# Two more weight blocks in vacated homes, a third layout of homes, and a rearranged first expert round

## The chip, the cores and the metric

One core of one Trainium2 chip runs the whole kernel in one launch. The metric is the device time of that core in microseconds (us), the median of several executions. The kernel before takes 501.85 us in the median of three (500.89 to 502.28).

## The reference

A graph attention network of two layers over 128 nodes of 768 features (4096 edges and a self-loop for each node), and after it a mixture of eight experts with a small tridiagonal solve at the end. Everything is float32. Cut to what matters here:

```python
h   = gat_conv(layernorm(x), W1 [768 x 6144], 8 heads)      # then elu
x   = x + gat_conv(elu(h), W2 [6144 x 768], 1 head)
xn  = layernorm(x)
probs = softmax(xn @ Wg + bg);  top_p = max(probs);  comb = one_hot(argmax(probs)) * top_p
h   = gelu(einsum('bnd,edh->ebnh', xn, W1) + b1)              # 8 experts, 768 x 3072 each
y   = einsum('ebnh,ehd->ebnd', h, W2) + b2                    # 8 experts, 3072 x 768 each
ffn = einsum('ebnd,bne->bnd', y, comb)
v   = clip(ffn @ Wv + bv); mask = scores >= 12th largest score; (gr, gi) = diagonal of a tridiagonal inverse of v
out = x + ffn + bk_scale * (clip(stack(gr, gi) * mask) @ Wo + bo)
```

The weights are some 190 MB and each is used once.

## The kernel before

The weights pass through SBUF in blocks. The GNN's come as 32 blocks of 1152 KB (`slot`), through a ring of nine slots. Each of the eight experts is a **round** of 14 blocks: six blocks of W1, 128 rows of 3072 numbers (1536 KB, index 0 to 5, the "upper" ones), and eight of W2 (1152 KB, index 6 to 13, the "lower" ones). A place in SBUF where a block lands is called a home.

**Homes.** While the GNN still runs, nothing but its ring and what it no longer needs is to be had, so the first round (round 0) has a layout of its own: `chunks` (chunk0 to chunk5) and `lowers` (lower0 to lower7, eight of the nine ring slots). From the second round (round 1) on there is another: `chunks_on` is three homes outside that area (extra0 to extra2) and chunk0 to chunk2, and `lowers_on` is three homes cut from chunk3 to chunk5 and then lower0 to lower4. So lower5, lower6 and lower7 fall vacant when round 0 is over. The kernel before puts rows and small tiles for the end of the program there.

**Who issues.** All weights are requested by SyncE's DMA queue (SPq), in program order. Ahead of each request SyncE waits on the semaphore `used`, which TensorE raises once for each block that it has read: by 32 over the GNN, and then by 14 a round. `used_after(r)` is 32 + 14 r. `load_round(r, e, first)` requests the blocks from `first` on of round r, and block i waits for `used` to reach `used_after(r - 1) + i + 1 - first`. For round 1, whose blocks 0 to 2 go to the extras ahead of that, `first` is 3: block 3 waits for the first block of round 0 to be read, and the last, 13, for the eleventh. For rounds 2 to 7 `first` is 0: block 0 of a round waits until TensorE has read block 0 of the round before.

```python
load(1, 1, 2, moe_in, chunks_on, lowers_on)
load_round(1, 1, first=3)
with sp.Fori(2, ROUNDS) as r:
    load_round(r, r)
```

**TensorE in a round.** `up(k)` multiplies block k of W1 by the gathered nodes (`gathered`, up to 64 nodes of that expert) into PSUM banks 0 to 2; ScalarE copies these to `upper`; `turn_upper(q)` transposes a quarter; VectorE adds the bias (`add_bias`), ScalarE takes the gelu; `down(q)` multiplies with two lower blocks into bank 4. `used` goes up at the end of up(0) to up(4), for block 5 at the first transpose of turn_upper(0), and at the end of each lower block. Beside that stand `gather` (it collects the nodes of the next expert), a transpose of `place_top` and `scatter` (it adds the last round's result into banks 6 and 7).

Round 0 has its own order, as the routing of nodes to experts is still being worked out in it: between its up's stand the rank products, the second half of the first gather, the turn of the scores, of `hot_top` (for `first_ffn`, the experts' b2) and of `place_top`. All this is in `round_(0, first=True)` of each engine. Between the GNN and round 0 TensorE has a chain of small steps with VectorE and ScalarE (second attention, sum, layer norm, gate). `stay_warm(n)` are n products of 128 x 128 that nobody reads, and `WARM` holds their numbers; `WARM[3]` are those ahead of the turn of the second attention's weights.

Of the kernel before, what the change touches and what calls it, by code (L numbers as in the profile page):

```python
# [19 lines left out]
P = 128  # L20
# [37 lines left out]
WARM = (3, 5, 2, 2, 2, 0, 1, 3, 2, 0, 8, 12)  # L58


def gnn_moe_kernel(nc, x, src, dst, gw1, gas1, gad1, gb1, gw2, gas2, gad2, gb2,
# [7 lines left out]
    with ctx:  # L69
        ctx.enter_context(nc.allow_non_contiguous_dma(reason="the gate's columns, 768 words each"))  # L70

        def sem(name):
            return ctx.enter_context(nc.semaphore(name))
# [51 lines left out]
        junk = nc.alloc_sbuf_tensor_at("junk", [P, D], f32, offset=moe_base + lower_at[5])  # L125
        top[0] = moe_base + lower_at[6]
        wo_rows = place("wo_rows", [P, 2, D])
        wv_row = place("wv_row", [P, D])
        top[0] = moe_base + lower_at[7]
# [9 lines left out]
        assert top[0] <= moe_base + lower_at[7] + slot  # L139
# [21 lines left out]
        chunks_on = [extra0, extra1, extra2] + chunks[0:3]  # L161
# [72 lines left out]
        lead_in = [sem(f"lead_in{i}") for i in range(LOADS)]  # L234
        up_done = sem("up_done")
# [63 lines left out]
        def _(sp):  # L299
# [35 lines left out]
            def load_round(r, e, first=0):  # L335
                for i in range(first, LOADS):
                    sp.wait_ge(used, used_after(r - 1) + i + 1 - first)
                    load(r, e, i, moe_in, chunks_on, lowers_on)

            for n in range(GNN_HALVES):  # L340
# [12 lines left out]
                if n == 22:  # L353
                    sp.wait_ge(spread, HEADS + 1)
                    sp.wait_ge(bias_done, 1)
                    sp.wait_ge(hot_ready, 4)
                    load(1, 1, 1, moe_in, chunks_on, lowers_on)
# [7 lines left out]
                if n == 25:  # L365
                    sp.wait_ge(x_based, 1)
                    load(1, 1, 0, moe_in, chunks_on, lowers_on)
# [27 lines left out]
        def _(pool):  # L395
# [51 lines left out]
            pool.wait_ge(used, used_after(0) + LOADS)  # L447
# [25 lines left out]
        def _(act):  # L473
# [67 lines left out]
            act.wait_ge(hot_turned, 1)  # L541
            S.copy(hot_T[:, :], ps[0:EXPERTS, 7, 0:P]).then_inc(hot_T_ready, 1)

            def round_(r, first=False):
# [8 lines left out]

                if not first:
                    take_y(r)
                act.wait_ge(place_turned, r + 1)
                S.copy(place_T[:, :], ps[:, 5, HB:512]).then_inc(place_T_ready, 1)
                for s in range(3):
                    take_upper(s)
                for q in range(QU):  # L560
                    gelu(q)

# [18 lines left out]
        def _(dve):  # L581
# [299 lines left out]
            def round_(r, first=False):  # L881
                def add_bias(q):
# [8 lines left out]
                dve.wait_ge(place_turned, r + 1)  # L891
                V.tensor_scalar(place_top[:, :], slot_no[:, :, :].rearrange("p a j -> p (a j)"),  # L892
                                rank[:, bass.ds(r + 1, 1)], col(TOPP), ALU.is_equal, ALU.mult)
                V.tensor_scalar(place_now[:, :], slot_no[:, 0, :], rank[:, bass.ds(r + 1, 1)], col(RSTD),
                                ALU.is_equal, ALU.mult).then_inc(place_ready, 1)
# [121 lines left out]
        def _(pe):  # L1017
# [239 lines left out]
            def round_(r, first=False):  # L1257
                upper_homes, lower_homes = (chunks, lowers) if first else (chunks_on, lowers_on)

                def landed(i):  # L1260
                    if first:
                        pe.wait_ge(lead_in[i], 16)
                    else:
                        pe.wait_ge(moe_in[i], 16 * r)
# [40 lines left out]
                if first:  # L1305
                    pe.wait_ge(first_gathered, 1)
                    up(0)
                    pe.wait_ge(onehot_ready, 1)
                    T.matmul(ps[:, 7, 16:24], later[:, :], hot, start=True, stop=True).then_inc(rank_done, 1)
                    T.matmul(ps[:, 6, 16:24], ones[:, :], hot, start=True, stop=True).then_inc(rank_done, 1)  # L1310
                    gather_first(3, KT, 5)
                    pe.wait_ge(first_gathered, 2)
                    up(1)
# [5 lines left out]
                    up(2)  # L1319
                    first_ffn()  # L1320
                    pe.wait_ge(first_gathered, 3)
                    up(3)
                    pe.wait_ge(thr_ready, 1)
                    T.transpose(ps[:, 5, HB:512], place_top[:, :], ident[:, :]).then_inc(place_turned, 1)
                    up(4)
                    up(5)
                else:
                    pe.wait_ge(gathered_ready, r)
                    up(0)
                    scatter(r)  # L1330
                    up(1)
                    up(2)
                    T.transpose(ps[:, 5, HB:512], place_top[:, :], ident[:, :]).then_inc(place_turned, 1)  # L1333
                    for k in range(3, KT):
                        up(k)
# [9 lines left out]
                if first:  # L1345

                    T.matmul(ps[:, 3, HB:HB + 1], ones[0:1, :], top16[0:1, KEEP - 1:KEEP], start=True,
                             stop=True).then_inc(thr_done, 1)
# [15 lines left out]
            with pe.Fori(1, rounds) as r:  # L1364
                round_(r)
# [63 lines left out]
```

## Time and profile before

| | |
|---|---|
| median of three executions | 501.85 us (500.89 to 502.28) |
| the profiled execution, its time | 502.62 us |
| its span in the trace | 500.8 us |
| TensorE busy | 466.2 us, 93% |
| VectorE, ScalarE, GpSimd busy | 136.2, 62.1, 32.9 us |
| read from HBM | 189.62 MB, 379 GB/s over the span |
| the weights' queue, share of 16 DMA engines | 93.2% |

The time exceeds the span by 1.8 us, which lie around the first and the last instruction. TensorE's busy share says little by itself: a product that waits for a semaphore behind its weight load, or whose end is modelled, counts as busy. What a DMA moved in each stretch is the more telling column here.

### The profile page before, as it was taken

To read this page: it belongs to the slowest core of one execution; us is meant where nothing else is said; L and a number is where in the kernel's file an instruction comes from. 1 tells how busy PE (TensorE), PEld (TensorE's weight loads), DVE (VectorE), ACT (ScalarE), POOL (GpSimd) and SP (SyncE) were. 2 spreads that over 40 slices of the span, in tenths; PEclk is the share of its full clock that TensorE was granted. 3 is DMA by queue.
4 is the path that set the end of the run, shared out by engine and by line. 5 is a ranking of instruction groups with operands and counts; after the bars stand their busy time and mean duration, and the time that the engine had idled before them with its cause. 6 is when DMAs were issued, how large, how long until landed. Compare 5 with 4: busy or idle time off the path is not lost.

```text
span 500.8 us, 5998 instructions
## 1 busy us (share of the span) xinstructions
PE 466.2 (93%) x2292; PEld 232.7 (46%) x2292; DVE 136.2 (27%) x362; ACT 62.1 (12%) x119; POOL 32.9 (7%) x52
## 2 busy tenths in 40 slices
PE   7999999999998999999999999999898889789892
PEld 6666665666556344344344344353243234224352
DVE  6673697437105311010010010010010011001165
ACT  1010222002003120020020020020020011002100
POOL 3242220000100000121000000000000000000000
PEclk9999999999998999999999999999999999999996
DMA  8889999999999699899999999999999999999800
GB/s 309 309 285 403 402 401 417 413 401 411 426 425 370 237 407 375 338 417 420 425 428 423 422 427 427 423 421 430 424 424 424 425 425 423 425 425 424 347 1 31
DMA packets 32541, 190.22 MB, mean 380 GB/s; under 512 B 5423, under 2 KB 5631, under 8 KB 18190
## 3 DMA queue, kind: packets, MB, share of 16 engines
q1 hardware_dynamic: 31694, 189.94, 93.2%
q8 instruction: 9, 0.15, 0.1%
q0 software_dynamic: 544, 0.05, 0.1%
q10 hardware_dynamic: 288, 0.03, 0.0%
q14 instruction: 6, 0.05, 0.0%
HBM read 189.62 MB, written 0.39 MB: 379 GB/s over the span
## 4 chain that ended last, share of the span: by engine, by line
PE 58%; DMA 22%; SPq 13%; DVE 5%; issue 2%; ACT 0%; DVEq 0%
PE ps L1300 16%; DMA chunk<-in_L_ffn_W 14%; PE ps L1273 14%; PE ps L1099 11%; PE ps L1059 6%; DMA lower<-in_L_ffn_W 6%; SPq L333 5%; SPq L323 4%; SPq L328 3%; PE ps L1286 2%; PE ps L1087 2%; DMA slot<-in_L_gnn_W 2%; PE ps L1114 2%; PE ps L1235 2%; SPq L347 1%
## 5 line engine op out<-in xcount | busy, mean ns | idle before, releaser
L1300 PE MATMUL ps<-lower,hidden 128*64 128x384 f32 x516 | 88.6, 490 | 5.3 <-DMA lower<-in_L_ffn_W 5.3
L1273 PE MATMUL ps<-chunk,gathered 128*64 128x512 f32 x324 | 73.5, 598 | 7.3 <-DMA chunk<-in_L_ffn_W 7.3
L1059 PE MATMUL ps<-slot,xT 128*128 128x384 f32 x192 | 64.0, 487 | 0.2 <-DMA slot<-in_L_gnn_W 0.2
L1273 PE MATMUL ps<-extra,gathered 128*64 128x512 f32 x252 | 57.6, 597 | 6.1 <-DMA extra<-in_L_ffn_W 5.9
L1300 PEld LDWEIGHTS ps<-lower,hidden 128*64 128x64 f32 x516 | 35.9, 137 | 51.2 <-issue 40.6
L1099 PE MATMUL ps<-slot,eluT 128*128 128x384 f32 x168 | 55.3, 486 | 0.0
L884 DVE TENSOR_TENSOR hidden<-ps,b_T 128x384 f32<-128x384 f32 x32 | 17.1, 555 | 129.8 <-PE ps L1286 129.8
L1059 PEld LDWEIGHTS ps<-slot,xT 128*128 128x128 f32 x192 | 35.6, 190 | 22.8 <-issue 0.3
L1273 PEld LDWEIGHTS ps<-chunk,gathered 128*64 128x64 f32 x324 | 21.7, 136 | 50.6 <-issue 36.7
L1300 PE MATMUL ps<-lower_on,hidden 128*64 128x384 f32 x252 | 43.7, 492 | 0.0
L1099 PEld LDWEIGHTS ps<-slot,eluT 128*128 128x128 f32 x168 | 31.5, 190 | 20.7
L892 DVE TENSOR_SCALAR place_top<-slot_no,rank,small 128x128 f32<-128x128 f32 x8 | 2.8, 346 | 130.6 <-PE ps L1333 126.5
L1273 PEld LDWEIGHTS ps<-extra,gathered 128*64 128x64 f32 x252 | 16.9, 136 | 42.5 <-issue 29.9
L551 ACT ACTIVATE hidden<-hidden 128x384 f32<-128x384 f32 x32 | 16.3, 523 | 79.7 <-DVE hidden L884 79.7
L1300 PEld LDWEIGHTS ps<-lower_on,hidden 128*64 128x64 f32 x252 | 16.9, 136 | 18.8 <-issue 17.5
L547 ACT COPY upper<-ps 128x512 f32<-128x512 f32 x24 | 14.0, 585 | 57.8 <-PE ps L1273 57.8
L1286 PEld LDWEIGHTS ps<-ident,upper 128*128 128x128 f32 x96 | 12.8, 199 | 16.1 <-issue 9.6
L658 DVE CUSTOM_DVE_ANT_0 xc<-h_sb,att_rows 128x768 f32<-128x768 f32 x16 | 16.5, 1033 | 9.6 <-issue 5.6
L1029 PE MATMUL ps<-ident 128*128 128x128 f32 x82 | 15.2, 343 | 2.9 <-DVE ident L601 2.9
L1286 PE MATMUL ps<-ident,upper 128*128 128x128 f32 x96 | 17.4, 304 | 0.0
L1029 PEld LDWEIGHTS ps<-ident 128*128 128x128 f32 x82 | 13.8, 253 | 4.0 <-DVE ident L601 2.9
L493 ACT ACTIVATE elu_e<-elu_e 128x384 f32<-128x384 f32 x16 | 8.4, 523 | 42.6 <-DVE elu_e L694 42.6
(303 smaller groups left out, 287.1 us busy)
## 6 DMA issues: line engine op xcount, KB each, us to landing
lower<-in_L_ffn_W SPq DMA_DIRECT2D x43, 1152.0 KB, 23.1
chunk<-in_L_ffn_W SPq DMA_DIRECT2D x27, 1536.0 KB, 19.7
slot<-in_L_gnn_W SPq DMA_DIRECT2D x31, 1152.0 KB, 15.6
extra<-in_L_ffn_W SPq DMA_DIRECT2D x21, 1536.0 KB, 25.1
lower_on<-in_L_ffn_W SPq DMA_DIRECT2D x21, 1152.0 KB, 28.7
slot<-in_L_gnn_W SPq DMA_DIRECT2D x3, 384.0 KB, 4.8
x_sb<-in_x SPq DMA_DIRECT2D x1, 384.0 KB, 3.4
out<-xc SPq DMA_DIRECT2D x1, 384.0 KB, 2.3
```

Of the source, the lines that this page charges most:

```text
L323: sp.dma_start(target, view).then_inc(small_in, 16)
L328: sp.dma_start(upper_homes[i][:, :], w1[e, i * P:(i + 1) * P, :]).then_inc(landed[i], 16)
L333: sp.dma_start(lower_homes[i - CHUNKS][:, :, :], view).then_inc(landed[i], 16)
L551: S.activation(hidden[:, q, :, :, :], hidden[:, q, :, :, :], ACT.Gelu_apprx_tanh).then_inc(gelu_done, 1)
L658: dot = V.tensor_tensor_reduce(out=xc[:, :], in0=h_sb[:, h, :], in1=att_rows[:, h % 2, j, :], scale=1.0, scalar=0.0, op0=ALU.mult, op1=ALU ...
L884: V.tensor_tensor(hidden[:, q, :, :, :], ps[:, q, 0:HB].rearrange("p (k b j) -> p k b j", k=3, b=2), b1_T[:, bass.ds(r, 1), :] .rearrange( ...
L1029: T.matmul(ps[:, bank, 0:P], ident[:, :], ident[:, :], start=True, stop=True)
L1059: last = T.matmul(ps[:, 2 * (h % 2) + b, 0:HB], xT[:, 3 * half + k, :], slots[n % RING][:, k, b * HB:(b + 1) * HB], start=(n % 2 == 0 and ...
L1099: last = T.matmul(ps[:, b, 0:HB], elu_part(KT * h + 3 * half + k, 1)[:, 0, :], slots[n % RING][:, k, b * HB:(b + 1) * HB], start=(h == 0 a ...
L1273: last = T.matmul(ps[b * CAP:(b + 1) * CAP, s, 0:BANK], gathered[:, k, :], upper_homes[k][:, at:at + BANK], start=(k == 0), stop=(k == KT ...
L1286: last = T.transpose(ps[:, q, k * P:(k + 1) * P], upper[:, q * HB + k:(q + 1) * HB:3], ident[:, :])
L1300: last = T.matmul(ps[c * CAP:(c + 1) * CAP, 4, 0:HB], hidden[:, q, k, b, :], lower_homes[i][:, k, c * HB:(c + 1) * HB], start=(i == 0 and ...
```

## The change

Five things.

1. `left0` and `left1`, two homes of 1536 KB, are laid over lower5, lower6 and two thirds of lower7, and SyncE requests blocks 0 and 1 of round 2 into them as soon as `used` reaches `used_after(1) - 1` and `used_after(1)`, the last two reads of round 0. The rest of round 2 (`load_round(2, 2, first=2)`) then waits two reads less for each block than before.
2. From round 2 on there is a third layout: upper homes left0, left1, extra0 to extra2, chunk0; lower homes `lower_late0` and `lower_late1` (cut from chunk1 and chunk2), the three cut from chunk3 to chunk5, and lower0 to lower2. What falls vacant is lower3 and lower4, after round 1, and the tiles for the program's end move there; GpSimd starts on them a round later. From round 3 on a round's block i waits again for block i of the round before.
3. Round 1, with the second layout and semaphores of its own (`second_in`), is written out apart from the loop on TensorE and SyncE.
4. Round 0 is rearranged on TensorE, VectorE and ScalarE: gather's second half ahead of up(1), the ranks ahead of up(2), the score ahead of up(3); the turns of `place_top` and `hot_top`, the gather for round 1 and `first_ffn` go behind down(0) and down(1), and all four `turn_upper` ahead of down(0).
5. `WARM[3]` is 8 and was 2.

The lines of the diff that the text speaks of:

```diff
-WARM = (3, 5, 2, 2, 2, 0, 1, 3, 2, 0, 8, 12)
+WARM = (3, 5, 2, 8, 2, 0, 1, 3, 2, 0, 8, 12)
...
+        left = [nc.alloc_sbuf_tensor_at(f"left{i}", [P, HID], f32, offset=moe_base + lower_at[5] + i * 4 * row)
+                for i in range(2)]
...
-        chunks_on = [extra0, extra1, extra2] + chunks[0:3]
+        chunks_2nd = [extra0, extra1, extra2] + chunks[0:3]
+        lowers_2nd = lowers_on
+        chunks_on = left + chunks_2nd[0:4]
+        lowers_on = [nc.alloc_sbuf_tensor_at(f"lower_late{i}", [P, 3, D], f32, offset=moe_base + chunk_at[1 + i])
+                     for i in range(2)] + lowers_2nd[0:6]
...
-            load(1, 1, 2, moe_in, chunks_on, lowers_on)
-            load_round(1, 1, first=3)
-            with sp.Fori(2, ROUNDS) as r:
+            load(1, 1, 2, second_in, chunks_2nd, lowers_2nd)
+            load_round(1, 1, second_in, chunks_2nd, lowers_2nd, first=3)
+            for i in range(2):
+                sp.wait_ge(used, used_after(1) - 1 + i)
+                load(2, 2, i, moe_in, chunks_on, lowers_on)
+            load_round(2, 2, first=2)
+            with sp.Fori(3, ROUNDS) as r:
                 load_round(r, r)
...
-            pool.wait_ge(used, used_after(0) + LOADS)
+            pool.wait_ge(used, used_after(1) + LOADS)
...
+                if not first:
+                    next_place()
                 add_bias(0)
                 add_bias(1)
-                take_gathered(r + 1, 5)
+                if not first:
+                    take_gathered(r + 1, 5)
                 add_bias(2)
+                add_bias(3)
                 if first:
+                    next_place()
+                    take_gathered(1, 5)
                     take_threshold()
-                add_bias(3)
...
-                    pe.wait_ge(gathered_ready, r)
-                    up(0)
...
+                    up(2)
...
+                    pe.wait_ge(first_gathered, 3)
+                    for k in range(3, KT):
+                        up(k)
+                    for q in range(QU):
+                        turn_upper(q)
+                    pe.wait_ge(thr_ready, 1)
+                    down(0)
                     pe.wait_ge(top_ready, 1)
+                    T.transpose(ps[:, 5, HB:512], place_top[:, :], ident[:, :]).then_inc(place_turned, 1)
+                    down(1)
...
+                    pe.wait_ge(place_ready, 2)
+                    pe.wait_ge(place_T_ready, 1)
+                    gather(5)
                     first_ffn()
-                    pe.wait_ge(first_gathered, 3)
-                    up(3)
...
+                    down(2)
+                    down(3)
```

On TensorE, in the middle of round 0, the kernel before has the following order. `chunk_69` to `chunk_72` are the upper blocks 2 to 5, `lower_73` and `lower_74` the first two lower blocks; `place_now` marks the gather, `b_sb,hot_T` `first_ffn`, `ident,upper` the turns.

```order
L1315 MATMUL ps<-ident,small 1x128
L1317 MATMUL ps<-ident,hot_top 8x128
L1273 MATMUL ps<-chunk_69,gathered 64x512 x6
L1254 MATMUL ps<-b_sb,hot_T 128x384 x2
L1273 MATMUL ps<-chunk_70,gathered 64x512 x6
L1324 MATMUL ps<-ident,place_top 128x128
L1273 MATMUL ps<-chunk_71,gathered 64x512 x6
L1273 MATMUL ps<-chunk_72,gathered 64x512 x6
L1286 MATMUL ps<-ident,upper 128x128 x6
L1235 MATMUL ps<-place_now,x_120 128x64 x6
L1300 MATMUL ps<-lower_73,hidden 64x384 x6
L1300 MATMUL ps<-lower_74,hidden 64x384 x6
```

After the change the same engine has, from the same product of the scores on:

```order
L1342 MATMUL ps<-ident,small 1x128
L1299 MATMUL ps<-chunk_70,gathered 64x512 x6
L1299 MATMUL ps<-chunk_71,gathered 64x512 x6
L1299 MATMUL ps<-chunk_72,gathered 64x512 x6
L1312 MATMUL ps<-ident,upper 128x128 x12
L1326 MATMUL ps<-lower_73,hidden 64x384 x6
L1326 MATMUL ps<-lower_74,hidden 64x384 x6
L1351 MATMUL ps<-ident,place_top 128x128
L1326 MATMUL ps<-lower_75,hidden 64x384 x6
L1326 MATMUL ps<-lower_76,hidden 64x384 x6
L1353 MATMUL ps<-ident,hot_top 8x128
L1258 MATMUL ps<-place_now,x_122 128x64 x6
```

The upper blocks 3 to 5 and the first lower blocks have moved ahead of `hot_top`, `place_top`, the gather and `first_ffn`. Nothing was added between them.

On SyncE, at the seam of round 1 and round 2, the kernel before has the last requests of round 1 and then those of its loop, each behind a wait for `used` (the ISA and REGISTER_ALU rows are the loop's register work):

```order
L333 DMA lower_76<-in_L_ffn_W 128x2304
L333 DMA lower_77<-in_L_ffn_W 128x2304
L381 UNCONDITIONAL_BRANCH
L381 ISA
L328 ISA
L328 DMA extra_119<-in_L_ffn_W 128x3072
L337 REGISTER_ALU
L328 ISA
L328 DMA extra_116<-in_L_ffn_W 128x3072
L337 REGISTER_ALU
L328 ISA
```

And after the change:

```order
L340 DMA lower_76<-in_L_ffn_W 128x2304
L340 DMA lower_77<-in_L_ffn_W 128x2304
L335 DMA left_84<-in_L_ffn_W 128x3072
L335 DMA left_85<-in_L_ffn_W 128x3072
L335 DMA extra_121<-in_L_ffn_W 128x3072
L335 DMA extra_118<-in_L_ffn_W 128x3072
L335 DMA extra_139<-in_L_ffn_W 128x3072
L335 DMA chunk_67<-in_L_ffn_W 128x3072
L340 DMA lower_late_140<-in_L_ffn_W 128x2304
L340 DMA lower_late_141<-in_L_ffn_W 128x2304
```

The two homes `left_84` and `left_85` now stand behind the last request of round 1, and the extras have become the third to fifth home of round 2.

## Rows read from the trace of the kernel before

**Rows 1.** The page, 40 slices of 12.5 us: GB/s that the DMA engines moved

```profile
GB/s 309 309 285 403 402 401 417 413 401 411 426 425 370 237 407 375 338 417 420 425 428 423 422 427 427 423 421 430 424 424 424 425 425 423 425 425 424 347 1 31
```

**Rows 2.** Stretches: length, busy times of PE, PEld, DVE, ACT, POOL, PEclk, DMA share, GB/s

```profile
155.16:158.58 3.42, 3.35 (x13) 2.18 (x11) 2.24 (x6) 1.85 (x5) 0.39 (x1) 0.50 0.99 361
157.00:170.00 13.00, 12.93 (x77) 7.87 (x77) 4.89 (x28) 3.49 (x9) 0.60 (x1) 0.94 0.69 253
170.00:195.00 25.00, 25.00 (x135) 10.91 (x133) 6.20 (x20) 3.76 (x8) 0.00 (x0) 1.00 0.94 360
195.00:204.00 9.00, 9.00 (x54) 3.59 (x50) 0.00 (x0) 0.77 (x2) 2.01 (x10) 1.00 0.97 407
204.00:216.00 12.00, 12.00 (x57) 4.00 (x57) 0.57 (x2) 0.27 (x1) 2.79 (x11) 1.00 0.90 347
240.00:316.00 76.00, 76.00 (x414) 31.39 (x414) 6.53 (x14) 9.06 (x18) 0.00 (x0) 1.00 1.01 426
316.00:445.00 129.00, 114.49 (x604) 44.55 (x600) 9.80 (x21) 13.60 (x27) 0.00 (x0) 1.00 1.01 424
```

**Rows 3.** The page, requests of one kind: count, KB each, median us to landing

```profile
lower<-in_L_ffn_W SPq DMA_DIRECT2D x43, 1152.0 KB, 23.1
chunk<-in_L_ffn_W SPq DMA_DIRECT2D x27, 1536.0 KB, 19.7
```

**Rows 4.** SyncE's requests in time: start, us from first to last, line, home

```profile
156.62 0.33 SPq L328 DMA_DIRECT2D extra<-in_L_ffn_W  x1
...
165.19 7.57 SPq L328 DMA_DIRECT2D chunk<-in_L_ffn_W  x3
176.63 6.19 SPq L333 DMA_DIRECT2D lower_on<-in_L_ffn_W  x3
186.45 9.76 SPq L333 DMA_DIRECT2D lower<-in_L_ffn_W  x5
204.41 6.46 SPq L328 DMA_DIRECT2D extra<-in_L_ffn_W  x3
...
237.86 0.33 SPq L333 DMA_DIRECT2D lower<-in_L_ffn_W  x1
...
240.45 0.34 SPq L328 DMA_DIRECT2D extra<-in_L_ffn_W  x1
```

**Rows 5.** TensorE ahead of the second attention's turn: start, us, what, [idle before]

```profile
151.21 0.61 PE L1029 MATMUL ps<-ident 128*128 128x128 f32 x4
153.46 0.33 PE L1076 MATMUL ps<-ident,att_p 128*128 128x128 f32 x1 [1.64 <-DVE small L782]
```

**Rows 6.** Pieces of the chain that ended last, in time: start, us, what

```profile
154.55 2.05 PE ps L1210 x4
...
157.30 0.90 PE ps L1021 x3
...
162.42 2.73 PE ps L1273 x12
...
165.69 0.72 PE ps L1242 x6
...
172.39 1.48 PE ps L1254 x4
...
183.04 1.29 PE ps L1235 x12
184.33 4.02 PE ps L1300 x24
188.35 0.54 PE ps L1286 x3
...
201.65 2.57 PE ps L1273 x12
```

**Rows 7.** The page, groups in the rounds: busy us, mean ns of one, idle before

```profile
L884 DVE TENSOR_TENSOR hidden<-ps,b_T 128x384 f32<-128x384 f32 x32 | 17.1, 555 | 129.8 <-PE ps L1286 129.8
L551 ACT ACTIVATE hidden<-hidden 128x384 f32<-128x384 f32 x32 | 16.3, 523 | 79.7 <-DVE hidden L884 79.7
```

More of the change, by code:

```diff
@@ L138, in gnn_moe_kernel @@
          cf_d, cf_c, cf_g, cf_e, cf_f, cf_pre, cf_px, cf_sx) = [place(*t) for t in tail_tiles]
-        assert top[0] <= moe_base + lower_at[7] + slot
+        assert top[0] <= moe_base + lower_at[4] + slot
         top[0] = after_moe
@@ L234, in gnn_moe_kernel @@
         lead_in = [sem(f"lead_in{i}") for i in range(LOADS)]
+        second_in = [sem(f"second_in{i}") for i in range(LOADS)]
         up_done = sem("up_done")
@@ L552, in gelu, with turn_place @@
                                  ACT.Gelu_apprx_tanh).then_inc(gelu_done, 1)
+                def turn_place():
+                    act.wait_ge(place_turned, r + 1)
+                    S.copy(place_T[:, :], ps[:, 5, HB:512]).then_inc(place_T_ready, 1)
                 if not first:
                     take_y(r)
-                act.wait_ge(place_turned, r + 1)
-                S.copy(place_T[:, :], ps[:, 5, HB:512]).then_inc(place_T_ready, 1)
+                    turn_place()
                 for s in range(3):
@@ L561, in round_ @@
                     gelu(q)
+                if first:
+                    turn_place()
+                    act.wait_ge(hot_turned, 1)
+                    S.copy(hot_T[:, :], ps[0:EXPERTS, 7, 0:P]).then_inc(hot_T_ready, 1)
             def take_y(n):
@@ L1255, in first_ffn, with round_ @@
                              start=True, stop=True)
-            def round_(r, first=False):
-                upper_homes, lower_homes = (chunks, lowers) if first else (chunks_on, lowers_on)
+            def round_(r, first=False, second=False):
+                upper_homes, lower_homes = ((chunks, lowers) if first else (chunks_2nd, lowers_2nd) if second
+                                            else (chunks_on, lowers_on))
                 def landed(i):
@@ L1262, in landed @@
                         pe.wait_ge(lead_in[i], 16)
+                    elif second:
+                        pe.wait_ge(second_in[i], 16)
                     else:
-                        pe.wait_ge(moe_in[i], 16 * r)
+                        pe.wait_ge(moe_in[i], 16 * r - 16)
                 def up(k):
@@ new lines, in round_ @@
+                    down(3)
+                    T.matmul(ps[:, 3, HB:HB + 1], ones[0:1, :], top16[0:1, KEEP - 1:KEEP], start=True,
+                             stop=True).then_inc(thr_done, 1)
+                    return
+                pe.wait_ge(gathered_ready, r)
+                up(0)
+                scatter(r)
+                up(1)
+                up(2)
+                T.transpose(ps[:, 5, HB:512], place_top[:, :], ident[:, :]).then_inc(place_turned, 1)
+                for k in range(3, KT):
+                    up(k)
@@ L1344, in round_ @@
                 turn_upper(3)
-                if first:
-                    T.matmul(ps[:, 3, HB:HB + 1], ones[0:1, :], top16[0:1, KEEP - 1:KEEP], start=True,
-                             stop=True).then_inc(thr_done, 1)
                 down(2)
@@ L1363, in _ @@
             rounds = pe.value_load(route[0:1, 0:1], min_val=ROUNDS, max_val=ROUNDS + 1)
-            with pe.Fori(1, rounds) as r:
+            round_(1, second=True)
+            with pe.Fori(2, rounds) as r:
                 round_(r)
```

45 lines of the change are left out of this document (16 added, 29 removed).

## The prediction, made before the changed kernel ran

> **What bounds the kernel now.** I read first what the DMA engines moved over the 40 slices [rows 1]. From slice 17 to 37 they move 417 to 430 GB/s without a break: the weights come as fast as this trace ever shows. So a byte that moves earlier ahead of that stretch ends the stream earlier, and the last expert's products and the final solve hang on the stream's end. Time is lost where the line of requests was short: in the first three slices (309, 309, 285), which the change leaves alone, and in slices 13 to 16 (370, 237, 407, 375, 338), between the GNN and the second expert round.
>
> Then the stretches [rows 2], counted against 425 GB/s: 157 to 170 us moves 253, a loss of 13 x (1 - 253/425) = 5.3 us; 170 to 195 moves 360, 3.8 us; 195 to 204 moves 407, 0.4 us; 204 to 216 moves 347, 2.2 us. Together 11.7 us. TensorE shows no idle in 158 to 216, so it is not waiting for weights; the weights wait for homes, which TensorE frees. Later, from 240 to 316 us, both columns are full (426 GB/s, TensorE 76.00 of 76.00) and from 316 on TensorE has pauses while the DMA does not: by then the stream alone decides. The requests in time [rows 4] show the holes: after 156.62 none until 165.19, and after 196.21 (186.45 + 9.76, less 0.33 for the start of the last: 195.88) none until 204.41, which is the first block of round 2, waiting for the first read of round 1.
>
> **An account of the stream.** An upper block of 1536 KB (1.573 MB) takes 3.70 us at 425 GB/s, a lower one of 1152 KB (1.180 MB) 2.78 us [rows 3]. I let a block start when the one ahead is through, but not sooner than 1.5 us after its request, and feed it with the 13 requests from 156.62 to 204.41 [rows 4], the line being empty at 157.1 us. Its idle time is 1.0 us after 156.62, 4.9 before the block of 165.19, 1.8 in small holes from 169 to 196 and 4.1 before that of 204.41, 11.8 in all against the 11.7 measured. The 1.5 us is my choice to make the two agree; with 1.0 it gives 11.3, with 2.1 12.4. It places the loss less well than it sums it: it has 1.8 us in the middle where the rows have 3.8, and more at both ends.
>
> **Part 1, the six warm products.** TensorE sits idle for 1.64 us ahead of the turn of the second attention, and its granted clock then is 0.50, the 1.2 GHz level, from 155.16 to 158.58 [rows 2, 5]. Two warm products show as x4 and span 0.61 us, so six more take at most 1.8 us (the 0.61 holds a start-up that further ones in a queue need not pay): they fill the idle time and end as the weights arrive, at worst 0.2 us late. At the full level the two products of 384 columns take 1.48 us (L1254, same shape of result) and not 2.05, and three turns 0.54 and not 0.90 [rows 6]. That is 0.57 + 0.36 = 0.9 us on the chain that leads to round 0. Bounds: nothing if the clock falls anyway, 1.7 us if all of the 3.42 us were products. I take 0.9, from the rows of the two groups on the chain.
>
> The Trainium skill ("TensorE: Matmul & The Clock Gate", Part 1 on the clock gate) says that the gate watches activity in a window that runs free of the kernel, and that the point of change therefore differs between runs. By that rule the filled gap need not help in each run, which is a rival below; this trace shows only one instance, at 155.16.
>
> **Part 2, the new order of round 0.** The pieces of the chain [rows 6] give the times of reads. up(0) moves from 162.42 to 161.5; each up is 2.73 or a little less, gather's half 0.72, `first_ffn` 1.48, the gather 1.29, a pair of lower blocks 4.02, the turn of a quarter 0.54 at most. The two rank products together, the score, and the turns of `place_top` and `hot_top` I take at 0.5, 0.3, 0.3 and 0.2, small products like the warm ones, of which two span 0.61 [rows 5]. In the new order SyncE's requests, each at the end of a read, come at 164.3, 167.8, 171.1, 174.1, 176.8, 179.7 (block 5), 183.2, 185.2, 187.4, 189.4 and 194.4 (block 10), where block 5 had been at 182.5 and block 10 at 195.9 [rows 4] (a span there ends 0.33 us after its last request goes out). The same work is done, so the round ends at about 200.7, 0.9 earlier than 201.65. Only the requests in between are 2 to 3.5 us earlier, because `first_ffn`, the gather and the two turns (1.48 + 1.29 + 0.5 us) now stand behind them.
>
> What could wait in it: down(0) follows the turns at once, with no gather between. The first bias (0.56 us) and gelu (0.52 us) [rows 7] need 1.1 us and two hand-offs after the first quarter is turned; the other three quarters are turned meanwhile, 1.4 to 1.6 us, so this costs 0 to 0.3 us. If that cover were gone, it would cost the whole 1.1. The vector work on the ranks, the top probability and the twelfth score, short steps on 128 x 8 and 1 x 128 numbers, has the up's of blocks 2 to 5 (11 us) to hide behind. I take nothing.
>
> **Part 3, two more homes.** Round 0's blocks 12 and 13 are read at about 198.3 and 200.3; the requests for left0 and left1 go out then, and the extras follow at 203.3, 206.8, 209.4. Before, they were 204.41 and two more by 210.9 [rows 4]. So the request at the hole comes 6.1 us earlier. In the account the middle has no idle left (before 1.8), the hole keeps 0.7 us (before 4.1), and the first part is 5.0 (before 5.9, as the earlier chain brings both requests forward). The line is never empty after that.
>
> Sum: 5.0 + 0 + 0.7 = 5.7 us of idle time where 11.8 was, a gain of 6.1. The rows bound it: if the middle gives 1.8 and the hole only what the rows show there, 0.4 + 2.2 - 0.7 = 1.9, it is 0.5 + 1.8 + 1.9 = 4.2 (and with the smaller 0.5 for the first part); with 3.8 in the middle and 3.4 at the hole it is 0.9 + 3.8 + 3.4 = 8.1. With only one or two blocks in line the rate is somewhat under 425 (the middle's 360 was not all holes), and the new middle is still such a stretch. So I take 5.7.
>
> **Part 4, what costs nothing.** The later start of GpSimd's end work (some 36 us later, still over 200 us ahead of the end) is off every path. TensorE's round 1, written out, has the same products. From round 3 on each request waits as before.
>
> The profiled execution would go from 502.62 to 496.9 us (span 500.8 to 495.1); it lies 0.8 above the median of the runs shown, so the median would be 501.85 - 5.7 = **496.1 us**.
>
> **The rivals.**
> *The clock falls all the same* (or falls at another place of this chain). For it: the fall is seen once, and the gap is filled only just. Then 0.9 us of the chain stays; in the account the idle time is 6.6, the gain 5.2, less the same 0.4: 497.0 us.
> *Round 0 pauses.* The new order brings products nearer to the vector and scalar work that they need. Each us ahead of block 0 or before the hole costs a whole us, since the line is empty there. 2 to 4 us of it give 498 to 500 us. Against it: the covers above.
> *Nothing is gained.* That takes another limit: homes scarce again at the next seam. TensorE reads a round in 36 us (201.65 to the like piece; requests 204.41 and 240.45 [rows 4]), a round's 18.9 MB takes 44.4 us. After the change no request goes out between the end of round 2's, at about 234, and the first of round 3, at about 239.3. The account's line is through at 244.2, so the new request is there (240.8 with its start) 3.4 us ahead of need; before it was 250.3 against 241.95. A margin of 3.4 us would have to go. That, or an unseen cap, would leave 501.9 us.
> *Slower.* One mechanism: ahead of block 0's read in round 0, where no cover exists, a stop of TensorE, such as warm products at the 1.2 GHz level that hold back the turn, or a wait for `gathered`'s second half ahead of up(1), which had a whole up to hide in and now has only up(0)'s end. The piece itself is 0.72 us and ScalarE's copy a fraction. It must exceed 5.7 us to decide, and 7.2 to be over 0.3% slower, ten times what these rows hold; it would give 503 to 505 us.
>
> **How the numbers follow.** Forecast 0.64 (its own range 494.4 to 497.8, from the bounds 4.2 and 8.1 drawn in to 7.5); clock 0.22; pause 0.08; nothing 0.04; slower 0.02. The range 494.5 to 498.2 holds the first two nearly whole. About 0.3% (1.5 us) is what a measurement can tell from no change. Faster by that: 0.64 + 0.22 + 0.08 = 0.94; within it 0.04; slower 0.02.
>
> **What would show it.** In the profile after: granted clock 1.00 in 155 to 159; requests at about 179.7 (block 8 of round 1), 194.4 and 198.3; a first hole of GB/s still there at 162 to 166, the middle over 400, and the hole at 203 to 206 gone; the stream's end some 5.7 us earlier. What would make me wrong: a middle that stays at 360 to 380 GB/s although requests come earlier, or waits in front of down(0).

## The result, and the profile after

The changed kernel takes 497.91 us in the median of six executions (496.13 to 498.67), the kernel before beside it 501.94 (six, 500.89 to 502.28). The ratio is 0.9913 with a 95% interval of 0.9901 to 0.9926: 4.0 us faster, and clear of no change. The profiled execution took 497.94 us with a span of 496.1; that of before had 502.62 and 500.8, so the two traces lie 4.7 us apart and not 4.0.

The page of the changed kernel, GB/s in 40 slices (here of 12.4 us), to be held against [rows 1]:

```profile
GB/s 292 332 274 403 401 401 414 413 405 409 426 424 412 291 401 398 384 429 418 424 422 423 426 427 425 424 424 424 424 424 427 427 421 425 425 426 424 338 0 32
```

The same stretches as in [rows 2]: length, busy PE, PEld, DVE, ACT, POOL, granted clock, DMA share, GB/s.

```profile
155.16:158.58 3.42, 3.26 (x23) 2.36 (x23) 2.02 (x6) 1.83 (x5) 0.60 (x1) 1.00 1.03 396
157.00:170.00 13.00, 13.00 (x77) 7.24 (x77) 3.64 (x25) 2.77 (x8) 0.60 (x1) 1.00 0.75 290
170.00:195.00 25.00, 24.85 (x133) 11.13 (x131) 6.14 (x19) 4.19 (x9) 0.00 (x0) 0.96 1.00 411
195.00:204.00 9.00, 9.00 (x52) 3.77 (x50) 0.45 (x2) 0.48 (x1) 0.00 (x0) 0.93 0.91 327
204.00:216.00 12.00, 12.00 (x57) 3.75 (x55) 0.57 (x2) 0.27 (x1) 0.00 (x0) 1.00 1.01 430
240.00:316.00 76.00, 76.00 (x414) 31.15 (x412) 6.53 (x14) 9.07 (x18) 5.19 (x17) 1.00 1.01 424
```

Against 425 GB/s the losses are now 13 x (1 - 290/425) = 4.1 us, 0.8, 2.1 and -0.1, 6.9 in all where before they were 11.7. The difference, 4.8 us, is the 4.7 us of the two spans: the whole gain lies between 157 and 216 us. It arrives at the other end through the stream: the products of the very last lower block wait for their DMA in both kernels, and start 4.71 us earlier (first row before, second after). From there both traces have 25.3 us more.

```profile
475.53 2.16 PE L1300 MATMUL ps<-lower,hidden 128*64 128x384 f32 x12 [0.51 <-DMA lower<-in_L_ffn_W]
470.82 2.16 PE L1326 MATMUL ps<-lower,hidden 128*64 128x384 f32 x12 [0.51 <-DMA lower<-in_L_ffn_W]
```

The middle has filled (360 to 411) and 204 to 216 is full; but 195 to 204, which before moved 407, moves 327. And the granted clock, 0.50 at 155 before and now 1.00 there, has another dent (a stretch at a lower granted clock), 0.96 and 0.93 further on.

SyncE's requests of the changed kernel around the two holes (start, us, line, home; each row is from a view of a short stretch):

```profile
155.83 0.33 SPq L335 DMA_DIRECT2D extra<-in_L_ffn_W  x1
163.92 0.33 SPq L335 DMA_DIRECT2D chunk<-in_L_ffn_W  x1
...
195.84 0.33 SPq L340 DMA_DIRECT2D lower<-in_L_ffn_W  x1
200.00 0.33 SPq L335 DMA_DIRECT2D left<-in_L_ffn_W  x1
201.93 0.33 SPq L335 DMA_DIRECT2D left<-in_L_ffn_W  x1
204.97 0.33 SPq L335 DMA_DIRECT2D extra<-in_L_ffn_W  x1
```

The homes are used as meant. Up to the middle the requests are 0.3 to 0.5 us ahead of the forecast (163.92 for 164.3); block 10's, block 12's and the extra's are 1.4, 1.7 and 1.7 us behind it (194.4, 198.3 and 203.3). What lies between them is in the chain of the changed kernel (start, us, what):

```profile
178.87 1.64 PE ps L1312 x12
180.50 0.15 issue
180.66 4.09 PE ps L1326 x24
184.75 0.26 PE ps L1351
185.01 4.02 PE ps L1326 x24
189.03 0.32 PE ps L1353 x2
189.34 1.48 PE ps L1258 x12
190.83 1.48 PE ps L1277 x4
192.31 9.59 PE ps L1326 x48
```

The last row is down(2) and down(3), blocks 10 to 13. By [rows 6] two such blocks take 4.02 us, four about 8; here they take 9.59. A stretch within it gives the reason:

```profile
193.00:196.00 3.00, 3.00 (x12) 1.23 (x10) 0.00 (x0) 0.00 (x0) 0.00 (x0) 0.50 1.00 421
```

TensorE runs at the 1.2 GHz level (0.50) from 193 to 196 us although it shows no idle time. Ahead of it stand the turn of `hot_top`, the gather (products of 64 columns) and `first_ffn` (8 rows of the array in use), which the new order has put next to each other. Whether they cause the fall is for the experiments.

### The profile page after: what moved, and what is told of

It is laid out like the page before. It is cut to its first block, busy times and chain, and to the rows that moved or that the text cites. A ratio compares the mean times of both kernels' runs of the same rounds, so it can differ in the third digit from the quotient of the medians.

```text
span 496.1 us, 5969 instructions
## 1 busy us (share of the span) xinstructions
PE 465.3 (94%) x2304; PEld 232.8 (47%) x2304; DVE 135.7 (27%) x362; ACT 62.0 (13%) x119; POOL 32.9 (7%) x52
## 4 chain that ended last, share of the span: by engine, by line
PE 73%; DMA 12%; SPq 6%; DVE 6%; issue 2%; ACT 0%; POOL 0%; DVEq 0%; POOLq 0%
PE ps L1326 19%; PE ps L1299 19%; DMA lower<-in_L_ffn_W 12%; PE ps L1082 11%; PE ps L1122 11%; SPq L340 6%; PE ps L1312 2%; PE ps L1110 2%; PE ps L1258 2%; PE ps L1137 2%; PE ps L1052 1%; PE ps L1388 1%; PE ps L1044 0%; DVE elu_y L708 0%; DVE cf_w L954 0%
## 5 line engine op out<-in xcount | busy, mean ns | idle before, releaser
L1326 PE MATMUL ps<-lower,hidden 128*64 128x384 f32 x372 | 65.2, 499 | 4.9 <-DMA lower<-in_L_ffn_W 4.7
L1326 PEld LDWEIGHTS ps<-lower,hidden 128*64 128x64 f32 x372 | 26.9, 139 | 40.6 <-issue 31.7
L1299 PE MATMUL ps<-chunk,gathered 128*64 128x512 f32 x180 | 40.8, 596 | 1.8 <-DMA chunk<-in_L_ffn_W 1.8
L1299 PE MATMUL ps<-left,gathered 128*64 128x512 f32 x144 | 33.3, 598 | 3.2 <-DMA left<-in_L_ffn_W 3.1
L1326 PE MATMUL ps<-lower_late,hidden 128*64 128x384 f32 x144 | 24.5, 490 | 0.0
L1299 PEld LDWEIGHTS ps<-chunk,gathered 128*64 128x64 f32 x180 | 12.3, 137 | 25.8 <-issue 21.9
L1299 PEld LDWEIGHTS ps<-left,gathered 128*64 128x64 f32 x144 | 9.6, 136 | 23.0 <-issue 17.3
```

The source lines that it names most:

```text
L1299: last = T.matmul(ps[b * CAP:(b + 1) * CAP, s, 0:BANK], gathered[:, k, :], upper_homes[k][:, at:at + BANK], start=(k == 0), stop=(k == KT ...
L1326: last = T.matmul(ps[c * CAP:(c + 1) * CAP, 4, 0:HB], hidden[:, q, k, b, :], lower_homes[i][:, k, c * HB:(c + 1) * HB], start=(i == 0 and ...
```

## The experiments

Theory: the stream of weights sets the time; it loses what TensorE's reads are late while its line is empty; the new order has a clock dent of its own that costs 1.7 us. The rivals: each part brings its own share wherever it stands; the shortfall against the account comes from a shallow line and not from the clock.

### The homes alone

The kernel before with edits 1 to 3 of the change and without 4 and 5:

```diff
-            with sp.Fori(2, ROUNDS) as r:
...
+            for i in range(2):
+                sp.wait_ge(used, used_after(1) - 1 + i)
+                load(2, 2, i, moe_in, chunks_on, lowers_on)
+            load_round(2, 2, first=2)
+            with sp.Fori(3, ROUNDS) as r:
```

> The kernel before with the extra homes and the third layout alone: round 0 in its old order, two warm products. If the gain is that of the hole ahead of round 2's first block, the first request for a left home goes out near 199.7 us and the second near 201.6 instead of 204.4, the stretch 204 to 216 moves over 420 GB/s and the middle (170 to 195) stays near 360. By the account of the stream that is 4.1 us less (11.8 to 7.7 us of idle time), by the rows of the hole at most 2.6: 497.8 to 499.3 us. Rival, that the new order is what matters and the homes only use what it frees: within 1 us of the kernel before.

Measured: 498.9 us (before beside it 502.0), ratio 0.9937 (0.9916 to 0.9958): 3.1 us. Stretches of this kernel, columns as above, and its requests for the left homes:

```profile
170.00:195.00 25.00, 25.00 (x137) 10.99 (x135) 5.69 (x17) 4.05 (x8) 0.00 (x0) 1.00 0.96 374
195.00:204.00 9.00, 9.00 (x52) 3.61 (x50) 0.00 (x0) 0.48 (x1) 0.00 (x0) 1.00 1.02 424
204.00:216.00 12.00, 12.00 (x57) 3.84 (x55) 0.57 (x2) 0.27 (x1) 0.00 (x0) 1.00 1.01 429
```

```profile
199.18 2.26 SPq L335 DMA_DIRECT2D left<-in_L_ffn_W  x2
```

The hole before round 2 is gone, the middle keeps most of its own. The gain falls between the rows' bound (2.6) and the account (4.1); its interval, 2.1 to 4.2 us, does not choose between them. Most of the change's 4.0 us is this part.

### The order alone

The changed kernel with the homes taken back. The eight warm products stay in it:

```diff
-        chunks_on = left + chunks_2nd[0:4]
-        lowers_on = [nc.alloc_sbuf_tensor_at(f"lower_late{i}", [P, 3, D], f32, offset=moe_base + chunk_at[1 + i])
-                     for i in range(2)] + lowers_2nd[0:6]
+        chunks_on = chunks_2nd
...
-            for i in range(2):
-                sp.wait_ge(used, used_after(1) - 1 + i)
-                load(2, 2, i, moe_in, chunks_on, lowers_on)
-            load_round(2, 2, first=2)
-            with sp.Fori(3, ROUNDS) as r:
+            with sp.Fori(2, ROUNDS) as r:
```

> The changed kernel without the extra homes: the new order of round 0 and the eight warm products stay, round 2's first block goes to its old home and waits again for round 1's first read. Theory: every earlier request only lets the line run dry earlier, since the stream can't restart before that read, which in the changed kernel comes at 205.0 us and before at 204.4. So it gives nothing or is up to 0.6 us slower than before: 501.5 to 502.5 us, middle over 400 GB/s, but a longer hole ahead of 205. Rival, that each part brings its own share: about 3.5 us less for the middle and 0.9 for the clock, near 498.

Measured: 502.33 us, ratio 1.0007 (0.9991 to 1.0022): no change. Its stretches:

```profile
170.00:195.00 25.00, 24.85 (x139) 11.55 (x139) 6.15 (x19) 4.20 (x9) 0.00 (x0) 1.00 0.99 405
195.00:204.00 9.00, 9.00 (x50) 3.44 (x48) 0.45 (x2) 0.48 (x1) 2.29 (x16) 1.00 0.57 218
```

The middle fills as in the changed kernel, and all of it is lost again behind it, most in 195 to 204 (218 GB/s), where no request goes out between these two:

```profile
193.65 0.33 SPq L336 DMA_DIRECT2D lower<-in_L_ffn_W  x1
202.64 0.36 SPq L331 DMA_DIRECT2D extra<-in_L_ffn_W  x1
```

Bytes moved earlier are worth something only if the line has others behind them. By the sum of [rows 2], the middle loses 1.2 us where it lost 3.8, and the stretches from 195 to 216 lose 5.2 where they lost 2.6.

This trace has the new order and no clock dent: its clock is 1.00 through all of round 0, and at 157 to 170 us it loses 3.5 us where the kernel before lost 5.3. Its span is 1.7 us under that of before, although the medians are the same. The twelve executions fall into two groups of six: 500.48 to 501.90 us with a mean granted clock of 0.989 to 0.992, the traced one among them, and 502.76 to 503.79 us with 0.987 or 0.988. So the dent probably comes in half of this kernel's executions; there is no trace of the second group, so this is not shown. The next experiment finds the warm products worth 1.0 us by themselves; here, with the order, nothing is left of that.

### The warm products: on the kernel before, and out of the changed one

```diff
-WARM = (3, 5, 2, 2, 2, 0, 1, 3, 2, 0, 8, 12)
+WARM = (3, 5, 2, 8, 2, 0, 1, 3, 2, 0, 8, 12)
```

> The kernel before with eight warm products instead of two, nothing else. Theory: in the kernel before the line restarts at the request that waits for round 1's first read (204.4 us), so whatever brings that read forward is gained whole: the clock stays 1.00 at 155, that request goes out near 203.1, and the time is 1.0 to 1.3 us less than before, near 500.8. Rival, that TensorE's chain ahead of round 0 is hidden behind the stream: no change.

Measured: 501.12 us beside 502.1, ratio 0.9982 (0.9972 to 0.9993): 1.0 us faster. The trace shows the clock at 1.00 around 155 and round 2's first request at 202.64 instead of 204.41 [rows 4]:

```profile
155.16:158.58 3.42, 3.25 (x26) 2.84 (x26) 1.94 (x7) 1.56 (x4) 0.60 (x1) 1.00 1.00 396
202.64 0.36 SPq L328 DMA_DIRECT2D extra<-in_L_ffn_W  x1
```

The request is 1.8 us earlier and the span 1.7 us shorter (499.1 for 500.8): nothing covers the chain ahead of round 0. The medians give less than the pair of traces. The traced execution of the kernel before has a mean granted clock of 0.985; of the 55 executions of it that ran beside the experiments 28 have 0.988 or less and take 502.2 us in the mean, 27 have 0.989 or more and take 501.3. So the fall at 155 seems to come in about half of them. This is a hint only, as the mean clock also counts falls near the program's end (0.78 from 484 to 488 us in the trace before).

The other way round, the changed kernel with `WARM[3]` at 2:

> The changed kernel with two warm products ahead of the second attention's turn instead of eight. Theory: TensorE then sits idle some 1.6 us there again, its granted clock is 0.5 for some 3.4 us around 155, the chain reaches round 0 0.9 to 1.3 us later, and since the line of requests is empty at 162 to 165 us and again ahead of the left homes, all of it is added: 1 to 1.3 us slower than the changed kernel, if the second fall (behind the gather) comes as in the changed kernel; if that one goes away, as the round lies elsewhere in time, the two nearly cancel. Rival, that the extra products only fill time: no difference, clock 1.00 at 155.

Measured: 497.37 us, ratio 0.9902 (0.9887 to 0.9918), against 497.91 and 0.9913 of the changed kernel: not slower, and the intervals overlap. The expectation's second branch came true: the request for left0 goes out at 199.87, in the changed kernel at 200.00. TensorE's wait and the clock's fall are back (timeline of TensorE, and a stretch), and the second dent is not there (chain):

```profile
153.74 0.33 PE L1099 MATMUL ps<-ident,att_p 128*128 128x128 f32 x1 [1.64 <-DVE small L798]
```

```profile
155.16:158.58 3.42, 3.35 (x11) 1.89 (x10) 2.48 (x7) 1.71 (x4) 0.00 (x0) 0.51 1.03 374
```

```profile
190.91 1.48 PE ps L1258 x12
192.39 1.48 PE ps L1277 x4
193.88 7.89 PE ps L1326 x48
```

Blocks 10 to 13 take 7.89 us here. So a dent costs 9.59 - 7.89 = 1.7 us of reads. The other traces that have these four blocks on end agree: 9.58 us with a dent (two repeats of the changed kernel), 7.89 without (four other kernels).

### Light pieces apart

`first_ffn` moved behind down(2) in the changed kernel:

```diff
                     gather(5)
-                    first_ffn()
                     down(2)
+                    first_ffn()
                     down(3)
```

> The changed kernel with first_ffn moved from behind the gather to behind down(2), so that the two light pieces of TensorE work no longer stand side by side. Theory one: their standing together (products of 64 columns and products with 8 rows in use, 3.3 us) is what sent TensorE's granted clock to 0.5 at 192.8 us, which made blocks 10 to 13 late by 1.7 us. Then the clock stays 1.00 in 189 to 200, the request for left0 goes out near 198.3 instead of 200.0, and the time falls by 1.2 to 2 us against the changed kernel, to about 496.2. Theory two: the fall has to do with something else (where in time the round lies), and the clock falls here too: then only the 1.5 us earlier blocks 10 and 11 are gained, under 0.7 us.

Measured: 496.87 us, ratio 0.9897 (0.9881 to 0.9913): 1.0 us less than the changed kernel, under the 1.2 to 2 expected, and the two intervals overlap. The gather starts at 189.65 us, within 0.3 us of where it does in the changed kernel. The clock stays 1.00, and the request for left0, at the end of block 12's read, is at 198.76.

```profile
157.00:170.00 13.00, 13.00 (x79) 7.45 (x80) 3.84 (x25) 3.09 (x8) 0.60 (x1) 1.00 0.75 287
170.00:195.00 25.00, 24.85 (x143) 11.08 (x139) 6.25 (x20) 4.20 (x9) 0.00 (x0) 1.00 0.98 409
195.00:204.00 9.00, 9.00 (x46) 3.66 (x46) 0.45 (x2) 0.48 (x1) 0.00 (x0) 1.00 0.99 389
```

Without the dent 195 to 204 moves 389 and not 327 GB/s.

### Dense work between them, light work between them

Six warm products (1.39 us in the trace) between the gather and `first_ffn`; and, in another kernel, the gather's six products done twice (1.34 us):

```diff
                     gather(5)
+                    stay_warm(6, 0)
                     first_ffn()
```

> The changed kernel with six more warm products of 128 x 128 between the gather and first_ffn, some 1.3 us of dense work that nobody reads. Theory one (light work side by side lowers the clock): the clock stays 1.00 in 189 to 200, so 1.7 us come back for the 1.3 us spent and the time is the changed kernel's less 0 to 0.5 us. Theory two (the light work is not the cause): the clock still falls and the requests for the left homes are 1.3 us later, the time 1.3 us longer than the changed kernel's.

Measured: 497.75 us, ratio 0.991 (0.9895 to 0.9926), clock 1.00 behind it (chain, and a stretch):

```profile
189.70 1.48 PE ps L1258 x12
193.00:196.00 3.00, 3.00 (x18) 1.24 (x18) 0.00 (x0) 0.00 (x0) 0.00 (x0) 1.00 1.00 417
```

The request for left0 goes out at 200.05, in the changed kernel at 200.00: the 1.4 us of added work are paid for by the clock that did not fall.

```diff
+                    for k in range(KT):
+                        T.matmul(ps[:, 5, k * CAP:(k + 1) * CAP], x1[:, k * P:(k + 1) * P],
+                                 place_now[:, :], start=True, stop=True)
                     gather(5)
                     first_ffn()
```

> The changed kernel with the six products of the gather done twice, so that the stretch of light TensorE work (hot_top's turn, gather, first_ffn) lasts some 4.6 us and not 3.3. The same time is added as by the six dense products, which left the clock at 1.00 and the time at 497.75. Theory one: the light work lowers the clock, so it falls to 0.5 behind it in nearly every execution, the left homes' requests are 1.3 us later than in the changed kernel, and the time is 1.3 us more than the changed kernel's (499.0 to 499.6), well over the dense version's. Theory two (the length of the piece or its place, not its lightness): as the dense version, 497.8.

Measured: 497.61 us, ratio 0.9918 (0.9902 to 0.9933), and no dent. The chain of this kernel shows 4.6 us of light work on end, and four blocks behind it under way at full clock:

```profile
188.76 1.48 PE ps L1358 x12
190.24 1.34 PE ps L1258 x12
191.58 1.48 PE ps L1277 x4
```

```profile
193.00:196.00 3.00, 3.00 (x21) 1.38 (x22) 0.00 (x0) 0.00 (x0) 0.00 (x0) 1.00 1.01 420
```

So theory one of this expectation (the light work lowers the clock, in nearly every execution) falls: more light work in one piece did not bring the dent, and all six executions took less than the 499.0 us that it asked for. Lightness alone is not the cause. The run does not separate the amount of light work from its place: here it starts at 188.76 us, 0.6 us earlier than in the changed kernel.

### The dent again, and round 0 moved in time

The changed kernel twice more:

> The changed kernel once more, for its clock: the fall behind the gather came in its one trace, but not in the trace of the kernel without the extra homes, whose round 0 has the same order. If it comes and goes from execution to execution, some repeats show 1.00 in 189 to 200 us and requests for the left homes near 198.3; if it is fixed to the order, each shows 0.5 there.

> The same as the repeat before it: one more execution of the changed kernel, for whether its clock falls behind the gather each time.

Both show the dent (a stretch of each, in this order), and took 499.25 and 498.98 us, one execution each, beside 501.48 for the kernel before. That is above all six executions of the first measurement, and 1.6 and 1.4 us above the median of the kernel with the gather done twice, which ran on the same chip:

```profile
193.00:196.00 3.00, 3.00 (x14) 1.21 (x12) 0.00 (x0) 0.00 (x0) 0.00 (x0) 0.55 1.01 424
```

```profile
193.00:196.00 3.00, 3.00 (x12) 1.23 (x10) 0.00 (x0) 0.00 (x0) 0.00 (x0) 0.50 0.99 414
```

Then six warm products ahead of round 0, which moves it as a whole:

```diff
-WARM = (3, 5, 2, 8, 2, 0, 1, 3, 2, 0, 8, 12)
+WARM = (3, 5, 2, 8, 2, 0, 1, 3, 8, 0, 8, 12)
```

> The changed kernel with six more warm products behind the rank product of the first expert (WARM[8] is 8 and not 2), ahead of round 0, so that the whole of round 0 comes 1.3 us later and is otherwise the same. If the clock's fall behind the gather hangs on where in time these pieces lie, as the traces so far suggest (three of three in the changed kernel, none where the same pieces come 0.8 us earlier or 1.3 us later), it stays away: the reads of blocks 10 to 13 gain 1.7 us and lose 1.3, and the time is the changed kernel's less 0 to 0.5 us, or at least no more. If it is fixed to the order of the pieces, the clock falls and the time is 1.3 us more, near 499.2.

Measured: 498.45 us, ratio 0.9932 (0.9912 to 0.9951). No dent:

```profile
190.03 1.48 PE ps L1258 x12
191.51 1.48 PE ps L1277 x4
```

```profile
193.00:196.00 3.00, 3.00 (x20) 1.39 (x22) 0.00 (x0) 0.00 (x0) 0.00 (x0) 1.00 1.01 420
```

The clock did as the expectation's first case said, the time did not: 0.5 us more than the changed kernel where it should have been no more. The two intervals overlap, and why the earlier request for left0 (198.99 us, in the changed kernel 200.00) gave nothing stays open.

In the traces with the gather and `first_ffn` adjacent and done once, the dent is there where the gather starts at 189.34, 189.67 and 189.46 us, all of one kernel, and not at 188.56 (order alone), 190.03 (this one) and 190.91 (two warm products), one trace each. With `first_ffn` moved away or dense products in between it is not there although the gather starts at 189.65 and 189.70, the place where the changed kernel has it. That fits a fall that hangs on both what stands side by side and when. But one trace of a kernel does not show what its other executions do: of the twelve of order alone six look as if they had the dent, and of the eight of the changed kernel seven have a mean granted clock of 0.985 to 0.987 and one, the fastest (496.13 us), 0.990. What tips it stays open.

### TensorE work once the line is full

On the kernel with `first_ffn` behind down(2), twelve products that nobody reads in round 1:

```diff
                 up(2)
+                if second:
+                    stay_warm(12, 4)
```

> The changed kernel with first_ffn behind down(2), and twelve more products of 128 x 128 that nobody reads in round 1 behind up(2), some 2.6 us of TensorE work. Theory: from the left homes' requests on the stream alone decides, and the seam of rounds 2 and 3 has some 4 us in hand, so it costs nothing: the time is that without them (496.9), within 0.4. Rival, that TensorE is still the bound up to 316 us, where it shows no idle time: 2.6 us more.

Measured: 496.94 us, ratio 0.99 (0.9884 to 0.9916), against 496.87 without them. The products are there, on the chain of the stretch:

```profile
209.63 2.88 PE ps L1052 x24
```

2.88 us of TensorE at 210 cost nothing, although TensorE shows no idle time up to 316 us; at 155 a chain 1.8 us shorter took 1.7 us off the span. The rival falls.

### The light pieces behind block 12

What the runs pointed to: bring block 12's read, which releases the first left home, forward, and keep the light pieces apart. `down(3, [0])` multiplies with the first of its two blocks only, `down(3, [1])` with the second.

```diff
+                    down(2)
+                    down(3, [0])
                     pe.wait_ge(place_ready, 2)
                     pe.wait_ge(place_T_ready, 1)
                     gather(5)
+                    down(3, [1])
                     first_ffn()
-                    down(2)
-                    down(3)
```

> The changed kernel with the gather behind block 12 and first_ffn behind block 13 (last in the round), so that blocks 10, 11 and 12 are read right behind block 9. Theory: the two light pieces are apart and the clock stays 1.00; the request for left0 goes out near 195.8 us (200.0 in the changed kernel, 198.8 with first_ffn behind down(2)), that for left1 near 199; the remaining dent of the stretch 195 to 204 (389 GB/s with first_ffn behind down(2)) goes to 415 or more. 0.3 to 0.8 us less than with first_ffn behind down(2), near 496.3. Rival, that the dent is the shallow line of single small blocks and not the late request: same as there, 496.9.

Measured: 495.9 us, ratio 0.9883 (0.9867 to 0.9898), the fastest of all: 2.0 us less than the changed kernel, with an interval just clear of its own, and 1.0 less than with `first_ffn` behind down(2), where the intervals overlap. The request for left0 goes out at 195.59, and the stretch is full:

```profile
195.59 0.33 SPq L335 DMA_DIRECT2D left<-in_L_ffn_W  x1
```

```profile
195.00:204.00 9.00, 9.00 (x50) 4.29 (x46) 1.01 (x3) 0.48 (x1) 0.00 (x0) 1.00 1.02 427
```

What the stream lost there came from the late request and not from a shallow line. What is left is the first hole (157 to 170 us).

## Why the prediction was right, and where it was off

**The bound** held: all the gain lies where the line of requests was short, and from 216 us on both kernels move the same. The slices are misnamed in the prediction: the five short ones (370 to 338) are 12 to 16, counted from 0, and the full ones end with 36.

**The sum** was off by 1.8 us (496.1 forecast, 497.9 measured; 497.9 lies 0.3 us inside the upper end of the range, which was drawn to hold the clock rival too, and just outside the likeliest case's own 494.4 to 497.8, whose upper end by its bound of 4.2 should read 497.65). The step that was mis-sized is in part 3: "the hole keeps 0.7 us". It rests on part 2's times for blocks 10 to 13, which took each pair at 4.02 us, TensorE at its full clock. The clock fell to 0.50 behind the gather and `first_ffn`, the four blocks took 9.59 us, block 12 was read at 200.0 and not 198.3, and the stretch 195 to 204 lost 2.1 us. Fed with the changed kernel's own requests, the prediction's account gives 7.4 us of idle time and not 5.7: 4.6 in the first part (5.0 forecast) and 2.8 at the hole (0.7 forecast). So its arithmetic held and the request times that it was given did not.

Only 1.0 of the 1.8 us shows in the traces (span 496.1, forecast 495.1). The rest is the step from the traced execution to the median: the forecast kept the 0.8 us by which the traced execution before lay above its median, and that of the changed kernel lies on its own (497.94 and 497.91).

With the two pieces apart the rows lose 4.2 + 0.9 + 0.8 - 0.1 = 5.8 us in the four stretches, against my 5.7 of idle time. In part that is luck: the first part was 0.8 too high and the middle 0.9 too low. Of the rivals it was the first, "or falls at another place", which I had priced at 497.0; but not on the chain ahead of round 0, which I had in mind, and dearer, 1.7 us and not 0.9. That two light pieces were being put side by side stood in the order and in my text, and I did not ask what they do to the clock.

**Part 1** was right in kind and, in the traces, too small: the clock stays full at 155, the eight products take 1.95 us and end 0.3 us ahead of the weights; the gather's first part starts 1.26 us earlier (160.34 against 161.60), not 0.9. The start of round 0 moves by itself from trace to trace, too: the request at the end of up(0) goes out at 163.13 to 164.27 us in ten traces with eight products (without the shifted one) and at 164.61 to 165.48 in three with two. By itself the part is worth 1.0 us. In the changed kernel it brought nothing measurable (497.37 without, 497.91 with): the trace without it has the first fall and not the second, the trace with it the second and not the first. The prediction's "only one instance" was a misreading: the trace before has more falls near its end (0.78 from 484 to 488 us).

**Part 2**: the middle filled (411) and down(0) waited 0.15 us, inside the 0 to 0.3. Not seen clearly enough: without the homes the order is worth nothing, even together with the warm products (1.0007).

**Part 3**: homes alone 3.1 us, account 4.1. Of the hole's 4.1 us in the account only 2.6 stood in the rows; I had noted that the account places the loss badly. The measurement is not sharp enough to say which was nearer.

**Part 4** held: the seam of rounds 2 and 3 shows 424 GB/s (no request starts between 234.56 and 241.16), and 2.9 us more of TensorE ahead of it cost nothing.

The rivals **pauses, nothing and slower**: none of them came.

The medians lie 4.0 us apart and the two traces 4.7. Single executions differ by up to 2.5 us in the changed kernel and 1.4 in the one before, more than these half microseconds; the rows of the stretches resolve them, but for one execution only.

## What to carry to other kernels

Where a stream of weights is the bound, draw up its line: each request with what it waits for, and when it is through. Work is worth moving only if it brings a request forward that meets an empty line; the same microsecond is free on one side of that point and costs all of itself on the other. Earlier requests in the middle were worth nothing here without more homes behind them; the homes alone gave 3.1 us, both with the warm products 4.0, and with the order fitted to the homes 6.2. When light TensorE work is gathered into one place, look at the granted clock behind it, and in more than one execution: a fall that comes in some of them makes the median a mixture.

## What the runs showed of the hardware that I had not expected

The granted clock fell to 0.50 with TensorE busy without a gap (stretch 193 to 196, 3.00 of 3.00 us busy), behind 3.3 us of products of 64 columns and products with 8 rows in use; in the changed kernel in three traces of three. In the one trace each of the kernels with the pieces 0.7 us later and 0.8 us earlier, with 1.4 us of dense products between the two pieces, and with 1.3 us more of light ones, it did not fall there. The times of order alone suggest that it comes in some executions and not in others. The Trainium skill ("TensorE: Matmul & The Clock Gate", Part 1) says that the gate's window runs free of the kernel. That fits a fall that comes and goes, but no run here shows the window itself.
